# Other order and sizes of the first loads, and a later step for one weight's norm, in a fused mixture-of-experts layer

## What is computed

```python
def mlp(x, gate_w, up_w, down_w):
    g = jnp.einsum('bsh,hi->bsi', x, gate_w)
    u = jnp.einsum('bsh,hi->bsi', x, up_w)
    return jnp.einsum('bsi,ih->bsh', jax.nn.gelu(g, approximate=True) * u, down_w)

w, sel = jax.lax.top_k(jax.nn.softmax(router_logits, axis=-1), 2)
w = w / w.sum(axis=-1, keepdims=True)
dense_w = jnp.zeros((B, E)).at[jnp.arange(B)[:, None], sel].add(w)
out = mlp(x, shared_gate, shared_up, shared_down)
for e in range(8):
    out = out + dense_w[:, e][:, None, None] * mlp(x, skill_gate[e], skill_up[e], skill_down[e])
return x + out
```

## Time and profile before

| | us |
|---|---|
| median of 3 runs | 210.87 |
| lowest and highest | 210.85, 211.42 |
| the profiled execution, whole | 211.93 |
| its span, first to last instruction | 210.1 |
| TensorE (PE) busy in the span | 205.2 (98%) |
| VectorE, ScalarE, GpSimd (POOL) busy | 123.6, 133.8, 117.9 |

### The profile page before, as it was taken

One profiled execution on the slowest core, in us unless ns is written; L12 is line 12 of the kernel. 1 busy time (PEld: TensorE's weight loads), 2 busy tenths in 40 slices (PEclk: granted clock), 3 DMA queues, 4 the chain that ended last, 5 costly groups with the idle time before them and its releaser, 6 DMA issues.

```text
span 210.1 us, 6672 instructions
## 1 busy us (share of the span) xinstructions
PE 205.2 (98%) x2695; PEld 165.0 (79%) x2695; DVE 123.6 (59%) x217; ACT 133.8 (64%) x217; POOL 117.9 (56%) x129
## 2 busy tenths in 40 slices
PE   7999999989999999999999999999999999999995
PEld 2444555445444478899999999999999999999995
DVE  2899657977999988554353444434435435344452
ACT  6283767677989997655656656556565565655650
POOL 3023644359548997665565655655656556565562
PEclk9999999999999999999999999999999999999999
DMA  6999600000000000000010010010010010010011
GB/s 196 391 433 434 296 2 0 0 3 0 2 0 5 0 0 3 0 3 5 3 53 3 0 53 3 3 53 0 3 55 3 3 53 0 3 53 4 3 50 53
DMA packets 2813, 11.70 MB, mean 56 GB/s; under 512 B 352, under 2 KB 608, under 8 KB 2400
## 3 DMA queue, kind: packets, MB, share of 16 engines
q1 hardware_dynamic: 2640, 11.01, 13.1%
q10 hardware_dynamic: 144, 0.26, 0.7%
HBM read 9.18 MB, written 2.10 MB: 54 GB/s over the span
## 4 chain that ended last, share of the span: by engine, by line
PE 93%; DVE 4%; issue 1%; ACT 0%; POOL 0%; POOLq 0%
PE o_ps L664 7%; PE g_ps L646 7%; PE u_ps L646 7%; PE o_ps L663 7%; PE u_ps L645 7%; PE g_ps L645 7%; PE u_ps L644 7%; PE g_ps L644 7%; PE o_ps L662 7%; PE u_ps L612 3%; PE g_ps L612 3%; PE g_ps L614 2%; PE o_ps L627 2%; PE o_ps L625 2%; PE o_ps L626 2%; PE g_ps L613 2%
## 5 line engine op out<-in xcount | busy, mean ns | idle before, releaser
L304 POOL TENSOR_TENSOR h<-h 128x512 f16<-128x512 f32 x92 | 109.2, 1194 | 79.2 <-ACT h L340 57.9
L457 DVE SCALAR_TENSOR_TENSOR h<-gel,sk_factor,u_ps 128x512 f32<-128x512 f32 x64 | 47.8, 747 | 68.0 <-PE u_ps L646 39.0
L335 ACT ACTIVATE gel<-g_ps,sk_gate 128x512 f32<-128x512 f32 x64 | 43.9, 687 | 49.8 <-PE g_ps L646 49.8
L340 ACT CAST h<-h 128x512 f16<-128x512 f32 x92 | 56.0, 609 | 3.5 <-DVE h L457 3.5
L645 PE MATMUL g_ps<-x,wsk 128*128 128x128 f16 x256 | 46.2, 219 | 0.0
L646 PE MATMUL g_ps<-x,wsk 128*128 128x128 f16 x256 | 46.2, 219 | 0.0
L645 PE MATMUL u_ps<-x,wsk 128*128 128x128 f16 x256 | 46.2, 219 | 0.0
L646 PE MATMUL u_ps<-x,wsk 128*128 128x128 f16 x256 | 46.2, 219 | 0.0
L644 PE MATMUL u_ps<-x,wsk 128*128 128x128 f16 x256 | 46.2, 219 | 0.0
L644 PE MATMUL g_ps<-x,wsk 128*128 128x128 f16 x256 | 46.2, 219 | 0.0
L663 PE MATMUL o_ps<-h,wsk 128*128 128x128 f16 x256 | 45.9, 219 | 0.0
(11 more groups left out here) (103 smaller groups left out, 310.1 us busy)
## 6 DMA issues: line engine op xcount, KB each, us to landing
wsk<-skills SPq DMA_DIRECT2D x3, 2048.0 KB, 16.1
outT<-xT SPq DMA_DIRECT2D x7, 256.0 KB, 2.0
xT<-xT SPq DMA_DIRECT2D x2, 768.0 KB, 6.3
wsh<-shared SPq DMA_DIRECT2D x3, 256.0 KB, 3.9
xT<-xT ACTq DMA_DIRECT2D x1, 256.0 KB, 3.5
xT<-xT SPq DMA_DIRECT2D x1, 256.0 KB, 4.6
outT<-xT SPq DMA_DIRECT2D x1, 192.0 KB, 2.6
outT<-xT SPq DMA_DIRECT2D x1, 64.0 KB, 1.5
```

The source lines that it names most:

```text
L304: nc.gpsimd.tensor_tensor(hidden_lo(t), hidden_full(t), hidden_hi(t), ALU.subtract).then_inc(lo_ok, 1)
L335: nc.scalar.activation(gel[:, t % NG, :], g_ps[t % 2][:, :], ACT.Gelu_apprx_tanh, scale=scale).then_inc(gelu_ok, 1)
L340: nc.scalar.copy(hidden_hi(t), hidden_full(t)).then_inc(hi_ok, 1)
L457: nc.vector.scalar_tensor_tensor(out=h32[:, t % N32, :], in0=gel[:, t % NG, :], scalar=factor, in1=u_ps[t % 2][:, :], op0=ALU.mult, op1=AL ...
```

## The change

All loads of weights and x go out on SyncE's (SP's) queue: group 0 of x first, then the first 128 columns of the shared gate and of the shared up weights with semaphores of their own (`chunk_in`), then the other 384 columns of each, down, and the rest as before. The router logits move to ACT's queue. TensorE's first GATE and UP wait for the chunks alone, its second for the whole weights. `zeros` is 128 columns wide instead of 512, and the warming matmuls read them four times over. The self-products of the skill down weights start at step 17 instead of 15, and five other entries of the tables of steps move with them.

```diff
-        zeros = sb("zeros", [P, GN], BF16)
+        zeros = sb("zeros", [P, P], BF16)
...
-        K_STEPS = [5, 10, 15]
-        MASK_AT = {3: X_NEXT, 9: K_GATE, 12: X_REST, 14: K_UP, 19: K_DOWN}
-        SPREAD_AT = {4: X_NEXT, 11: K_GATE, 14: X_REST, 16: K_UP, 21: K_DOWN}
+        K_STEPS = [5, 10, 17]
+        MASK_AT = {3: X_NEXT, 9: K_GATE, 12: X_REST, 15: K_UP, 21: K_DOWN}
+        SPREAD_AT = {4: X_NEXT, 11: K_GATE, 15: X_REST, 17: K_UP, 23: K_DOWN}
...
-        TABLE_AT = {4: X_NEXT, 15: X_REST}
-        SKILL_TABLES_AT = 23
+        TABLE_AT = {4: X_NEXT, 16: X_REST}
+        SKILL_TABLES_AT = 25
...
-            sp.dma_start(logits[:, :], cond).then_inc(cond_in, 16)
-            for q in (GATE, UP, DOWN):
-                sp.dma_start(wsh32[:, q * I:(q + 1) * I], shared[:, q * I:(q + 1) * I]).then_inc(sh_in[q], 16)
+            sp.dma_start(xT32[:, 0:GN], xT[:, 0:GN]).then_inc(x_in[0], 16)
+            for q in (GATE, UP):
+                sp.dma_start(wsh32[:, q * I:q * I + P], shared[:, q * I:q * I + P]).then_inc(chunk_in[q], 16)
+            for q in (GATE, UP):
+                sp.dma_start(wsh32[:, q * I + P:(q + 1) * I], shared[:, q * I + P:(q + 1) * I]).then_inc(sh_in[q], 16)
+            sp.dma_start(wsh32[:, DOWN * I:], shared[:, DOWN * I:]).then_inc(sh_in[DOWN], 16)
...
-            act.dma_start(xT32[:, 0:GN], xT[:, 0:GN]).then_inc(x_in[0], 16)
+            act.dma_start(logits[:, :], cond).then_inc(cond_in, 16)
...
                 dve.wait_ge(sh_in[q], 16)
+                if q < DOWN:
+                    dve.wait_ge(chunk_in[q], 16)
...
-                    nc.tensor.matmul(g_ps[1][:, :], zeros[:, 0:P], zeros[:, :], start=True, stop=True)
+                    nc.tensor.matmul(g_ps[1][:, :].rearrange("p (k s) -> p k s", k=C), zeros[:, :],
+                                     zeros[:, :].unsqueeze(1).broadcast_to([P, C, P]), start=True, stop=True)
...
             pe.wait_ge(x_in[0], 16)
+            pe.wait_ge(chunk_in[GATE], 16)
+            gate_up_first(0, GATE)
+            pe.wait_ge(chunk_in[UP], 16)
+            gate_up_first(0, UP)
             pe.wait_ge(sh_in[GATE], 16)
-            gate_up_first(0, GATE)
+            gate_up_first(1, GATE)
             pe.wait_ge(sh_in[UP], 16)
-            gate_up_first(0, UP)
-            gate_up_first(1, GATE)
             gate_up_first(1, UP)
```

More of the change, by code:

```diff
@@ L129, in build @@
         sh_in = [sem(f"sh_in{q}") for q in range(3)]
+        chunk_in = [sem(f"chunk_in{q}") for q in range(2)]
         sk_in = [sem(f"sk_in{q}") for q in range(3)]
```

## The result

The changed kernel takes 214.1 us, the median of 5 runs (213.68 to 215.89), beside 210.93 for the kernel before (5 runs, 210.85 to 211.42). The ratio is 1.0151, 95% interval 1.0117 to 1.0186: **slower by 1.5%**, some 3.2 us. The forecast was 210.6 with a range of 209.6 to 211.7.

A forecast was written before the change was run, and what follows sets the result against it. TensorE was taken as the bound (busy 205.2 of 210.1 us), VectorE second up to about step 31. Start -0.4, waits removed -1.5, waits added +1.6 give -0.3: 210.87 to 210.6 us, range 209.6 to 211.7.

The forecast's parts named there:

- The first matmul and the chunks: TensorE's first float32 matmul, waiting only for the 128-column weight chunks, starts at 4.40 us instead of 4.99.
- The pace of the loads: Weights and x at the start: 64 KB more costs 0.16 us, so group 1 of x lands by 7.4.
- The slack of 0.5 us at FIRST's mask: After the second UP: VectorE's mask of FIRST, moved to about 8.4, still comes 0.5 us before TensorE needs it.
- 1.06 us between the profiled execution and the median: Profiled 211.93 us against median 210.87: no term scales with the whole time, so differences are subtracted from the median.
- The start as a whole: Start of the kernel, from zeros and loads: -0.4 us, between -0.3 and -0.47.
- The rival that the clock rises earlier: Start: both first products take 0.86, TensorE then waits for FIRST's mask; -0.8 there, 210.2 us in all; chance 0.08.
- The start gives nothing: Start: chunks land near 5.0 with a gap before them; 0.0 there, 211.0 us in all; chance 0.12.
- The waits removed: TensorE's waits at X_REST's spread (0.5 us) and before the self-products after UP of step 15 (1.0) go: -1.5.
- The waits added: New TensorE waits in the moved steps: 0.3 + 0.2 + 0.2 + 0.8, rounded up to +1.6 us.
- K_UP's spread: After step 17's GATE and DOWN: TensorE waits 0.2 us for VectorE's K_UP mask, done at 45.5.
- The walk: Hand-overs between engines followed from step 14 to K_DOWN's spread in step 23, using old times, to find new waits.
- The port: Rival, step 15: POOL blocks VectorE's scales of X_REST behind `skill_low`; 1.0 us more, 211.6 in all; chance 0.15.

## Why the prediction was wrong, step by step

The forecast was -0.3 us and the result +3.2. About 2.7 of the 3.5 between them lie at the start, where -0.4 was forecast and about +2.3 measured, and about 0.9 in the steps, where it was +0.1 against +0.9 to +1.1.

**The first matmul and the chunks.** Forecast 4.40, measured 4.16 in after, and 4.25 and 4.37 in two more profiles with these loads. The matmuls on repeated columns cost what the others do. Right. The estimate from the Trainium skill (DMA: Bandwidth & Descriptors, section Bandwidth), a chunk at 5.2, is not borne out: TensorE used it at 4.16.

**The pace of the loads.** This is the step that failed first: the term for the loads, and with it FIRST's mask "at about 8.4", where it was measured at 10.73. I took 0.16 us for 64 KB, the pace at which the whole weights had landed one behind the other, and had 256 KB of group 1 of x land by 7.4. It landed at 10.0, and down at 8.0 where 6.4 was implied. The pace was 221 to 248 GB/s instead of about 400. I also held that an issue that goes out 0.9 later costs nothing as long as earlier transfers are still under way, and named "no second queue runs beside it" as a reason for an early landing. The runs show either as a loss: 0.6% for one queue, 0.6% for the chunks with their two extra issues.

**The slack of 0.5 us at FIRST's mask.** It was read from one execution, in which the first products ran at half clock until 7.0. In the profiles of down's self-products alone and of the scales first, which have the start of before unchanged, the first two products are 0.93 and 1.14 apart, and GATE of step 4 comes 0.8 and 0.9 earlier than in the profile of before. With the clock up early TensorE wants the mask at about 8.4, and the first of the two waits 0.3 for it, while the other asks 0.4 after it is ready. So most of the 1.06 us between the profiled execution and the median, which I carried through as a constant, was probably this, and little or none of the slack was left in such a run. That also closes the sum, as an estimate from these traces: against its profile the start lost 1.5 us where the clock didn't fall afterwards, against the median run 0.8 more, 2.3.

**The start as a whole:** -0.4 was forecast. Measured: 1.2% alone, 2.4 us, in four runs of which two had the fallen clock. The rival that the clock rises earlier had its premise right (first products at 0.93 and 0.86 in after) and its price wrong, for the same late mask. "The start gives nothing" was the nearest, and had no term for a loss.

**The waits removed.** -1.5 was right: from step 14 to 16 the distance falls by 1.97, which is 1.5 and the self-products of one step (0.46).

**The waits added.** In after, by the distances from start to start: POOL's rest 0.44 (forecast 0.3), K_UP's spread 1.2 (0.2, and 1.0 more in the rival), GATE(19) 0.2 (0.2), K_DOWN's spread 0.7 (0.8). Sum 2.5 against 1.6; minus 1.5 that is +1.0, against +0.9 read from the steps. The walk held in each hand-over, ACT's idle time and the wait for `hidden(16)` included.

**The port.** The rival given 0.15 came true as described: L419, released behind `skill_low`, starts 0.04 us after POOL and lasts 1.14. Its price of 1.0 was right. So the moved steps alone were the rival's +1.1 and not the forecast's +0.1. With the scales ahead of `skill_low` the same tables give -1.2 (-0.9 by the traces). Of the 2.4 us between (1.9 by the traces), 1.0 is read from the row as the port's share and the rest goes to the place behind `skill_low`, with what hung on it on ACT; only the two together are shown by a run, since none kept the place without the stall. That second part had been in my walk as the price of the change; it belonged to an order of two calls within a step, not to the step numbers.

**What stays open.** Why the last parts of group 1 of x land at 8.4 and 8.9 where group 0 went ahead of it on the same queue, and at 6.8 to 8.0 otherwise, with the bytes and its issue time the same; and why pieces of gate and up make down late where pieces of down don't, though both slow the stream.

## What to carry to other kernels

A load that is split or moved to be early for one consumer makes later loads late for another: before moving it, list each load's consumer with its slack, and take the slack from several executions, since a clock that rises late makes it look larger. A small instruction that another engine waits for should stand ahead of a long one in its engine's step, above all where the long one's end also releases POOL. A median run and a profiled run that differ by 1 us differ somewhere: find the place before carrying the difference through a sum.

## What the runs showed of the hardware

- **One queue was slower than two for the same bytes.** With whole weights, 312 GB/s from 6 to 8 us where group 0 went first on SP (272 behind the logits, 275 with the routing moved), 373 to 409 in six profiles with it on ACT's queue. A transfer is over when the last of its 16 parts is, and these spread: group 1's median part landed at 6.5 before and 7.9 after, its last at 7.2 and 10.0.
- **A small VectorE instruction can cost as much as POOL's long one beside it.** `i_bits` and `s_bits` of 128x3 take 0.16 us alone and took 1.14, 0.94, 0.56 and 0.48 with POOL's 1.16 us operation under way, always until POOL's end, while `e_bits`, which reads PSUM, took 0.15. Not every small one stalls: with one column instead of three, in the scales of K_UP, `i_bits` and `s_bits` took 0.15 beside POOL's, and in step 14 of before `s_bits`, which started 0.03 us ahead of POOL's second operation, took 0.15. The Trainium skill (SBUF — State Buffer, section SBUF: two separate sides) describes an exclusive lock for some forms of VectorE instruction, where the loser "fully blocks"; the trace agrees for the three-column forms, and shows it for a start only 0.04 us behind POOL's.
- **TensorE's clock rose at different times in the same program.** With nearly the same work ahead of them, the first two float32 products were 1.84 us apart in four profiles and 0.86 to 1.67 in the others. In the profiles the granted clock fell to 0.50 behind idle stretches of 2.6, 2.8 and 3.1 us, and stayed at 1.00 behind those of 1.35 and 1.39. It isn't the kernel alone that decides: by the mean clock (0.992) it fell in 1 of 5 runs of the changed kernel, 2 of 4 of its start alone and 6 of 11 with the scales first. Those runs took 1.3 to 2.4 us more than the others of the same kernel.
